# Batch 0's image rows made first from a copy of their own, and the patches of the other rows spread in parts among the first text chunks

## What is computed

```python
h = patches_of(x and four shifted copies) -> [32, 36, 3840]       # layernorm over 3840
h = normed @ W.T + b                                              # 36 image tokens a batch
h = concatenate([h, txt], axis=1)                                 # 164 tokens
# attention on layernorm(h):  k0, v0, g0 are those of batch 0 alone
retrieved = einsum('bhk,hkv->bhv', q_t, fw)
fw = 0.95 * fw + (0.1 * g0_t) * (k0_t outer v0_t)                 # one state for all batches
h = h + layernorm(h) + retrieved @ w_out.T
# experts on layernorm(h): rms norm, router, top 2 of 8
y = sum over the two experts of  down_e(silu(gate_e x) * up_e x) * weight
h = h + layernorm(h) + y
```

## Time and profile before

| | us |
|---|---|
| runs of the kernel: 613.36, 619.07, 621.52; median | 619.07 |
| the profiled execution's own time | 614.67 |
| its span in the trace | 612.9 |
| PE busy in the span | 501.1 (82%) |
| DVE busy | 363.5 (59%) |
| ACT busy | 296.8 (48%) |
| POOL busy | 186.7 (30%) |

### The profile page before, as it was taken

One profiled execution on the slowest core, in us unless ns is written; L12 is line 12 of the kernel. 1 busy time (PEld: TensorE's weight loads), 2 busy tenths in 40 slices (PEclk: granted clock), 3 DMA queues, 4 the chain that ended last, 5 costly groups with the idle time before them and its releaser, 6 DMA issues. The chain is left out here.

```text
span 612.9 us, 12751 instructions
## 1 busy us (share of the span) xinstructions
PE 501.1 (82%) x3132; PEld 469.3 (77%) x3133; DVE 363.5 (59%) x1235; ACT 296.8 (48%) x744; POOL 186.7 (30%) x270
## 2 busy tenths in 40 slices
PE   5999999997887868500999999999999999999300
PEld 2799998876775756400999999999999999999300
DVE  2658855365777655573466565655566665655286
ACT  0268864336567544451344444444444444444262
POOL 0000000005556655552133333333333333333300
PEclk9999999697889786755899999999999999999755
DMA  8992205511223322222222222222222222222299
GB/s 355 435 373 103 104 1 169 194 38 54 78 79 92 95 82 67 84 67 88 51 75 75 75 74 72 67 75 74 75 75 75 75 75 73 65 75 66 94 422 305
DMA packets 52028, 71.62 MB, mean 117 GB/s; under 512 B 18994, under 2 KB 45427, under 8 KB 50467
## 3 DMA queue, kind: packets, MB, share of 16 engines
q1 hardware_dynamic: 39632, 47.93, 24.6%
q0 software_dynamic: 8208, 16.95, 7.7%
q10 hardware_dynamic: 4162, 6.45, 2.8%
HBM read 49.43 MB, written 21.86 MB: 116 GB/s over the span
## 5 line engine op out<-in xcount | busy, mean ns | idle before, releaser
L688 POOL DMA_INDIRECT disp<-xf,posu x82 | 81.7, 997 | 196.5 <-ACT xf L579 164.1
L700 POOL DMA_INDIRECT ydram<-ysb,dnow x89 | 87.3, 981 | 69.4 <-POOL dnow L697 66.4
L1361 DVE TENSOR_TENSOR hh<-sg,bank 128x384 f32<-128x384 f32 x89 | 49.3, 554 | 94.2 <-ACT sg L641 94.2
L641 ACT ACTIVATE sg<-bank 128x384 f32<-128x384 f32 x89 | 43.7, 491 | 114.7 <-PE bank L966 114.7
L962 PE MATMUL bank<-wa,xh 128*128 x178 | 67.7, 380 | 0.0
L966 PE MATMUL bank<-wa,xl 128*128 x178 | 60.5, 340 | 0.0
L964 PE MATMUL bank<-wa,xl 128*128 x178 | 60.4, 339 | 0.0
L963 PE MATMUL bank<-wa,xh 128*128 x178 | 60.2, 338 | 0.0
L965 PE MATMUL bank<-wa,xh 128*128 x178 | 60.0, 337 | 0.0
L697 POOL COPY dnow<-dest 128x1 uint32 (+1 forms) x89 | 16.4, 184 | 123.5 <-DVE ysb L1371 123.5
L868 PE MATMUL pair<-nst,xT 96*128 96x208 f32 x164 | 45.3, 408 | 8.1 <-DVE posu L1264 8.0
(11 more groups left out here) (234 smaller groups left out, 1174.2 us busy)
## 6 DMA issues: line engine op xcount, KB each, us to landing
xs<-disp SPq DMA_DIRECT2D x89, 96.0 KB, 2.0
imgT<-in_pixels SPq DMA_DIRECT2D x4, 1536.0 KB, 17.8
band<-in_bands SPq DMA_DIRECT2D x4, 1536.0 KB, 12.8
yall<-ydram ACTq DMA_DIRECT2D x5, 768.0 KB, 13.2
hres<-in_text SPq DMA_DIRECT2D x1, 3072.0 KB, 34.1
wa<-in_gate_up_w SPq DMA_DIRECT2D x8, 384.0 KB, 8.5
ring<-in_gate_up_w SPq DMA_DIRECT2D x32, 96.0 KB
yall<-ydram SPq DMA_DIRECT2D x4, 768.0 KB, 13.3
```

The costliest lines, as they stand in the source:

```text
L688: pool.indirect_dma_start(disp, bass.IndirectOffsetOnAxis(ap=posu[c % XBUF][:, 2 * j + k:2 * j + k + 1], axis=0), xfd[c % XBUF][:, j, :], None
L700: pool.indirect_dma_start(ydram, bass.IndirectOffsetOnAxis(ap=dnow[b][:], axis=0), ysb[b][:], None).then_inc(s_ys[b], 16)
L1361: v.tensor_tensor(hh[o][:], sg[o][:], bank[2 * o + 1][:, 0:DE], ALU.mult).then_inc(s_hh, 1)
```

## The change

- The host hands over two more inputs: `pixels0`, the pixels of batch 0's 36 image tokens as matmul columns, and `features0`, the same tokens' 3840 features as 36 rows. PE makes the 36 tokens in one group of 24 matmuls with 36 stationary columns; ACT takes their squares in two instructions, and DVE norms them (`t0`, `h0`, `h0n`). With the text rows they give a whole `x0T`, so one projection, one gate and one set of products cover all of batch 0's 164 tokens. `pick`, `head_bank` and the products of the head are gone.
- Before that PE runs three quarters of patch 0, then five parts of 6 matmuls among the first `rows`, and then 7 parts in each of the first four chunks, 3 after the first two `present`, 4 after the last two. The patches go through two PSUM banks in turn, not four.
- The chunks run in the order 3 to 9, 2, 0, 1, 10. The states and rows of chunks 1, 2 (`nsti`) and 0 to 2 (`crowi`) are kept for later.
- The squares, the reading and the norming of patches, the statistics and the norming of tiles move into `turn(t)` of ACT and DVE, t = 0 to 21 by half-chunk. The units run at the turns of `UNIT_TURN`, six of the 28 before turn 9, the other 22 from turn 9 on. SP's loads are reordered around that.
- Some constants are set by POOL rather than DVE, and buffers are laid elsewhere (`wcT`, `aw`, `xs`, `x0`).

The core of the diff:

```diff
-EARLY = (0, 1, 2, 5, 6)
-LATE = (3, 4, 7, 8)
-PATCH_BANK = (0, 1, 5, 6)
-PROJ_BANK = (4, 7, 2, 3)
+PATCH_BANK = (2, 3)
+PROJ_BANK = (4, 6, 5, 7)
+ORDER = (3, 4, 5, 6, 7, 8, 9, 2, 0, 1, 10)
+LN_GROUPS = (range(12, 20), range(20, 28), range(28, 36), range(36, 41), range(8, 12), range(0, 8))
+STATS_TURN = (None, 0, 3, 7, 9, 10)
+PART = 6
+READ_TURN = (None, 0, 2, 3, 4, 5, 6, 7, 8)
+UNIT_TURN = (4, 4, 5, 6, 6, 7, 9, 9, 9, 10, 10, 11, 11, 12, 12, 13, 13, 14, 14, 15, 15, 16, 16, 17, 17, 18, 19, 21)
...
 @block.sync
+            sp.dma_start(img0[:], pixels0).then_inc(s_img0, 16)
+            sp.dma_start(feat0[:], features0).then_inc(s_feat0, 16)
...
+            sp.wait_ge(s_sq, 12)
+            sp.dma_start(band[0][:], bands[:, 2]).then_inc(s_band[2], 16)
+            sp.wait_ge(s_pat, 3)
+            main_in(EXPERTS[0])
...
 @block.scalar
+            def turn(t):
+                if t:
+                    add_norm(turn_norms(t))
+                if t + 1 < PTILES:
+                    squares(t + 1)
+                if t < PTILES:
+                    std_patch(t)
+                if t in STATS_TURN:
+                    std_text(STATS_TURN.index(t))
+                for n in turn_units(t):
+                    high(n)
...
+            for i in range(CHUNKS):
+                c = ORDER[i]
+                if i + 1 < CHUNKS:
+                    xT_out(i + 1, 0)
+                turn(2 * i)
+                if i + 1 < CHUNKS and nt(i + 1) > 2:
+                    xT_out(i + 1, 1)
+                if i > 1:
+                    norm2(i - 1)
+                if IMAGES <= c < CHUNKS - 1:
+                    state_out(c + 1)
+                turn(2 * i + 1)
...
+                if i:
+                    add_norm2(i - 1)
+                std2(i)
...
 @block.tensor
+            def patches(n):
+                for _ in range(n):
+                    p, part = divmod(next(part_n), PARTS_OF_PATCH)
+                    i, j = p // 3, p % 3
+                    if part == 0:
+                        pe.wait_ge(s_img[min(j, 1) if i == 0 else i + 1], 16)
+                        if p >= 2:
+                            pe.wait_ge(s_patout, p - 1)
...
+            for k in range(24):
+                ins = pe.matmul(bank[0][0:NPATCH, 0:193], img0[:, k, :], wcT[:, k, :], start=(k == 0), stop=(k == 23))
...
+            patches(3)
+            pe.wait_ge(s_x0n, 2)
...
+            patches(1)
+            pe.wait_ge(s_kvout, NH)
+            pe.wait_ge(s_vvout, NH)
+            rows(0)
...
                 last.then_inc(s_o, 1)
+                if i < 4:
+                    patches(3)
...
+                if i < 4:
+                    patches(4)
...
 @block.vector
+            def turn(t):
+                if 0 < t <= PTILES:
+                    patch_norm(t - 1)
+                if t in READ_TURN:
+                    patch_read(READ_TURN.index(t))
+                if t < PTILES:
+                    patch_var(t)
+                if t in STATS_TURN:
+                    stats1(STATS_TURN.index(t))
+                if t - 1 in STATS_TURN:
+                    scale1(STATS_TURN.index(t - 1))
...
+            for i in range(CHUNKS):
+                turn(2 * i)
+                for n in turn_units(2 * i):
                     low(n)
+                residual(i)
+                sums(i)
+                picks(i)
+                stats_2(i)
+                turn(2 * i + 1)
+                if i + 1 < CHUNKS:
+                    mask(i + 1)
+                places(i)
+                for n in turn_units(2 * i + 1):
                     low(n)
+                scale2(i)
```

More of the change, by code:

```diff
@@ L105, in link, with build @@
         self.wait()
-def build(nc, pixels, bands, text, W, bias, attn_w, par, norm_w, router_w, gu_w, down_w, consts, out):
+def build(nc, pixels, bands, pixels0, features0, text, W, bias, attn_w, par, norm_w, router_w, gu_w, down_w, consts, out):
     with ExitStack() as ctx:
@@ L530, in _ @@
+            act.wait_ge(s_vh0, 1)
+            nc.scalar.activation(p0[:, 10:11], p0[:, 9:10], ACT.Sqrt, bias=cst[0:NPATCH, C_EPS:C_EPS + 1]).then_inc(s_sdh0, 1)
+            for n in range(2):
+                key_projection(n)
+            nc.scalar.preload_act_table_set("sigmoid_and_others")
+            for h in range(4):
+                keys(h)
             act.wait_ge(s_gs, 1)
             nc.scalar.activation(kgate[:], gsum[:], ACT.Sigmoid).then_inc(s_g8out, 1)
+            for h in range(4, NH):
+                keys(h)
@@ L777, in turn @@
-            def turn(c, half):
-                tiles = range(4 * c + 2 * half, 4 * c + min(nt(c), 2 * half + 2))
+            pe.wait_ge(s_wqc, 1)
+            for hp in range(4):
+                for which in range(2):
+                    kv(which, hp)
+            def turn(i, half):
+                tiles = [tile(i, j) for j in range(2 * half, min(nt(i), 2 * half + 2))]
                 pe.wait_ge(s_h1, 1 + max(NORMED.index(t) for t in tiles))
-                if c or half:
-                    pe.wait_ge(s_xT, 2 * c + half)
+                if i or half:
+                    pe.wait_ge(s_xT, 2 * i + half)
@@ L833, in _ @@
-            text_kv(1, 1)
-            for m in range(2):
-                ins = pe.matmul(bank[3][:, 0:SPAD], wgR[:, m, :], x0T[:, m, :], start=(m == 0), stop=(m == 1))
-            ins.then_inc(s_g8, 1)
-            turn(0, 0)
-            text_kv(1, 2)
-            text_kv(1, 3)
-            for which in range(2):
-                pe.wait_ge((s_k0head, s_v0head)[which], 1)
-                pe.wait_ge(s_vvout, 6 + 2 * which)
-                for hp in range(4):
-                    head_kv(which, hp)
@@ L887, in _ @@
+            rows(0)
+            pe.wait_ge(s_st0, 1)
+            turn(0, 0)
+            patches(1)
+            rows(1)
+            state(0)
             turn(0, 1)
-            pe.wait_ge(s_kvout, NH + 2)
-            pe.wait_ge(s_vvout, NH + 2)
-            rows(0)
+            patches(1)
+            rows(2)
+            state(1)
             scores(0)
-            rows(1)
-            pe.wait_ge(s_st0, 1)
-            for c in range(CHUNKS):
-                if c + 1 < CHUNKS:
-                    turn(c + 1, 0)
+            patches(1)
@@ L897, in _ @@
+            rows(3)
+            state(2)
+            patches(1)
+            rows(4)
+            for i in range(CHUNKS):
+                c = ORDER[i]
+                if i + 1 < CHUNKS:
+                    turn(i + 1, 0)
                 pe.wait_ge(s_ns, c + 1)
                 pe.wait_ge(s_rows, 2 * c + 2)
[L899 to L905 removed]
@@ L922, in _ @@
+                if i + 1 < CHUNKS and nt(i + 1) > 2:
+                    turn(i + 1, 1)
+                if nt(i) > 2:
+                    if i:
+                        pe.wait_ge(s_pos, i)
+                    past(i, 2)
+                    present(i, 2)
+                    past(i, 3)
+                    present(i, 3).then_inc(s_o, 1)
+                if i < 4:
+                    patches(4)
+                if IMAGES <= c < CHUNKS - 1:
                     state(c)
-                if c + 2 < CHUNKS:
+                if IMAGES <= c < CHUNKS - 2:
@@ L1046, in _ @@
             v.tensor_copy(rwsc[:], router).then_inc(s_ns, 1)
-            st.link(v.tensor_copy(zrow[:, D + 1:DROW], cst[:, C_PAD:C_PAD + 2]))
-            mean, var, q = (sd2[:, 25 + k:26 + k] for k in range(3))
-            def patch_out(p):
+            st.wait()
+            st.mark(v.scalar_tensor_tensor(out=t0[:], in0=scb[0:NPATCH, 0, :], scalar=p0[:, 3:4], in1=bank[0][0:NPATCH, 0:D],
+                                           op0=ALU.mult, op1=ALU.add))
+            v.wait_ge(s_psd0, 1)
```

793 lines of the change are left out of this document (367 added, 426 removed).

## The result

The changed kernel took 634.75 us in the median of four runs (628.41 to 637.81), the kernel before 618.51 beside it (613.36 to 621.52): a ratio of 1.026, 95% interval 1.015 to 1.037. The profiled execution took 633.23 us, its span 631.4, against 614.67 and 612.9. So it is slower; whether by 2% isn't settled by these runs. Beside 585.7 the changed kernel took 613.5, a ratio of 1.050 (1.045 to 1.055).

A forecast was written before the change was run, and what follows sets the result against it. No engine is full in the chunks; PE, fullest up to the fifth router sums, was followed with waits for others. Last router sums at 274.9 instead of 266.8, 8.1 us later, on 614.67 give 622.8 us; range 600 to 636.

The forecast's parts named there:

- the case of no change or a little slower: Whole kernel: last chunk's router sums 8.1 us later, 622.8 us; the forecast itself, chance 0.50.
- z0 to z4: From the first chunk's router sums, at 88.0 us, to the fifth's, at 189.9: four periods with patch parts.
- Up to z0: Head until the first chunk's router sums: batch 0's patch 8.0 us, projection from 38.0, first router sums at 88.0.
- Waits for banks: Chunks 1 to 3 of the loop: PE waits for DVE to read patches from two banks, 11.4 us, between 0 and 18.
- Third period: Third to fourth router sums: patches 5 and 6 wait 3.8 and 2.1 us for banks, period 28.4 us.
- The fourth period: Fourth to fifth router sums: ACT's roots 17.6 us after `present`, then DVE's work, 23.0 us in all.
- z4 and z5: Fifth and sixth router sums at 189.9 and 208.4 us; the period between is DVE's, 18.5 us.
- Last chunks: Chunks without patches after the sixth router sums: 13.8 us each, tenth router sums at 263.4, last at 274.9.
- Rival of the filled holes: Chunks: ACT and DVE are as early as PE needs, so bank waits go: 601.1 us; chance 0.22.
- Rival of the longer scatter round: Late chunks: moved units lengthen the scatter's round to 15.9 us, four times 2.1 us more: 631.3 us; chance 0.20.
- Rival of the clock: Patch parts in the loop: bank waits bring PE's clock to 0.83, 18 us longer: 641 us; chance 0.08.

The follow-up runs named there:

- the early reading: Changed kernel with DVE reading every patch from 2 on out of its bank as soon as it is there: 601.19 us, ratio 1.029.
- second profile: Changed kernel run again unchanged in a later group, beside a kernel before at the 585 level: 613.50 us, ratio 1.050.
- ACT's list put in order: Changed kernel with banks read early, tiles normed before the state, second-layer roots earlier, text roots last in their turn, residual update later: 596.61 us, ratio 1.021.
- the experiment without parts: Changed kernel with the remaining 28 patch parts all run ahead of the first chunk, with DVE's and ACT's share: 638.05 us, ratio 1.089.
- the version with earlier patches: Changed kernel, ACT's list reordered, patches two turns further ahead, 12 parts instead of 5 before the loop: 620.30 us without interval; 617.6 us, ratio 1.005.

## Why the prediction was right, and where its steps were off

The time, 622.8 forecast, was 633.2 in the profiled execution, inside the range of 600 to 636 and near its upper end; the case of no change or a little slower was right in sign and 10 us short. The difference to the kernel before is a harder test: forecast 8.1 us, measured 16 in the medians of the first group and 28 at 585, where 13.8 us a chunk, the base of the sum, isn't the kernel's own pace. That the time fell into the range is in part luck of the level at which it was first taken.

By the marks, forecast and measured: z0 to z4 101.9 and 107.9 us, in periods 26.3, 28.4, 24.2 and 23.0 against 26.2, 29.4, 26.5 and 25.8.

- **Up to z0**: 88.0 forecast, 90.2 measured. Batch 0's patch took 9.5 us on PE at a clock of 0.84 and 8.06 at 1.00 (8.0 taken, 7 to 10 given), so the size was right and the clock was left out. z0 is 90.2 in both profiles, though the projection begins at 39.4 in one and at 37.8 in the other, for 38.0 forecast: in the second all of the 2.2 lies in the keys and rows behind it. That narrow stationary columns would not shorten the patch was right: its 48 matmuls took 327 ns in the median, the wide ones 326. The rule on weight loads by their columns, in the Trainium skill's "TensorE: Matmul & The Clock Gate", section LDWEIGHTS, shows in the load in part: 113 ns for 36 columns instead of 189 for 128, shorter, but not in proportion. The load didn't set the pace, so nothing of it reached the time. The experiment that leaves out 18 matmuls shows that the patch is on the path.
- **Waits for banks**: 3.8, 3.8, 2.1 and 1.7 us forecast, 11.4 in all; measured 3.0, 4.5, 1.3 and 1.85, 10.7 in all, and the early reading took 12.3 us off. (The terms that I listed for ACT in the second period add up to 15.7, not 16.3; the copy of the state itself, 0.5, isn't among them.) Mechanism and size were right: the step in which the read stands behind `scale2` and the norming. What a wait does to the clock was not in the sum: 1.75 us in the second period, which came out 1.0 longer than forecast.
- **Third period**: PE went from one last `present` to the next in 24.3 us, as forecast; DVE's router sums came 2.3 us later behind it, after two low units of which the first had waited 1.6 us for ACT.
- **The fourth period** is the step that failed. I let z4 follow ACT's roots by way of DVE, and had no wait of PE for normed tiles. Without holds (second profile) it took 20.6 us, less than forecast: PE waits 4.0 for tiles that ACT norms behind the residual's update and the roots, and z4 comes 0.7 us behind PE's last `present`. In the first profile a hold of 5.2 us on ACT's copy of the state came on top. ACT's list put in order, with the tiles ahead, took the period to 18.1.
- **z4 and z5**: the fifth period took 20.8 us, 18.5 forecast. DVE is busy 17.4 us of it, by the pieces I listed; moving some of its units moved the time into the period before.
- **Last chunks**: 56.5 us for four, 55.0 forecast; the last 9.1 instead of 11.5. This agreement is luck: the 13.8 a chunk was 9.8 of the kernel's own and 4 of holds. At 585 the changed kernel takes 45.5 us for the four and the kernel before 39.3. The sum of the terms: 2.2 + 6.0 + 2.3 + 1.5 - 2.4 = 9.6 us, which is 284.5 - 274.9.
- **Rival of the filled holes**: it needed a kernel before with holes of its own. The waits of ACT and DVE in its 13.8 us a chunk, which I read as room for patches, aren't there at 585 us: 9.8 a chunk, with 1.3 of PE free. Even with the bank waits gone the changed kernel stayed 2.9% slower.
- **Rival of the longer scatter round**: no. POOL's gaps from one chunk's last issue to the next one's first were 5.3, 3.6, 2.0 and 0.3 us between z5 and z10, not over 5.5 throughout.
- **Rival of the clock**: not at its size, 0.94 from z0 to z4. It fell to 0.76 behind z4, and to 0.73 over the first five periods of the experiment without parts. By the section "HAM oscillation" of the same page of the Trainium skill a loop that waits between its bursts pays in each round; the trace agrees for the chunks without parts. Of the first three periods with parts it bears it out in one (0.94, the others 1.00).

Why no gain at all, at 585 us, where both kernels are free of holds: z0 moves up by 42.9 us (133.1 - 90.2), for 50 us of patch parts taken out of the head; the 7 that are missing are about what batch 0's own patch costs. The parts then cost 50 us between z0 and z4, and 6 more come of waits and the clock (101.0 - 45.0 = 56.0). The fifth period adds 10.5, z5 to z9 6.3, the last gives back 0.4: -42.9 + 56.0 + 10.5 + 6.3 - 0.4 = 29.5, and z10 moved by 29.4, from 234.75 to 264.13. Work was moved from a stage in which PE was full into one in which PE had 1.3 us in 9.8 to give; what came with it (batch 0 twice, statistics and units that can't start before the last patch has freed its memory) was extra. With banks and ACT in order 12.4 us are left at z10 (247.2 against 234.75): z4 then comes 4.9 us earlier than in the kernel before (173.2 against 178.1), and what follows takes 17.3 longer.

What stays open: where the holds come from and what divides the two levels; whether the version with earlier patches is level at 585 us too; what the later turns of the units cost by themselves; how much of the late periods is units and how much statistics. No version beat the kernel before.

## What to carry to other kernels

Before work is moved to start a later stage sooner, add up what the fullest engine has to do in both stages together: here PE was busy 190.8 of the 213 us from 21.4 to z10 at 585, so some 22 were free, and no order of the same work could bring more than that, and 7 of them went to a second patch. An engine's waits in a profile are room only if they recur in another run of the same kernel; a wait whose releaser is not an engine of the kernel is the first to be doubted. When two engines' work is woven into a third one's holes, put what the third waits for (bank reads, normed tiles, roots) ahead of everything that nobody waits for: that was worth 17 of the 28 us lost at 585.

## What the runs showed of the hardware

Where holds show, ACT and DVE mostly go on 1.0 to 1.9 us behind the last scatter of a row of eight (the earlier trace rows has 217.65 to 219.32), although PE had long delivered: 13 of the 17 rows with a remote releaser in the chunks of the two first profiles lie so, one comes 0.04 us behind it, three within the row. In the changed kernel PE's state matmuls are over at 177.9 and its scores near 180.4; the last scatter is issued by 181.5:

```profile
177.04 0.84 PE L922 MATMUL bank<-crow,arow 128*96 128x200 f32 x4
...
178.44 1.96 PE L899 MATMUL bank<-xT,keysT 96*128 96x512 f32 x4
...
180.55 0.96 POOL L763 DMA_INDIRECT disp<-xf,posu  x1 [0.31 <-issue]
...
183.08 0.49 ACT L602 COPY nst<-bank 96x400 f32<-96x400 f32 x1 [10.85 <-remote]
183.23 0.69 DVE L1230 TENSOR_TENSOR sm<-bank,cst 128x512 f32<-128x512 f32 x1 [1.76 <-remote]
183.47 0.98 ACT L544 ACTIVATE hres<-hres,lt 128x192 f32<-128x192 f32 x2
...
184.51 0.67 PE L879 MATMUL bank<-ident,hres 128*96 128x128 f32 x4 [4.10 <-ACT hres L544]
```

ACT's copy of the state starts 5.2 us after PE's matmul. DVE's own work, which waits for no other engine, runs on through the scatters. The kernel before shows 41.2 us of such waits, ACT's and DVE's together, in one profile and none in another whose span is 30 us shorter. In both, a scatter takes 0.96 us in the median with 0.30 behind it, so the scatters themselves are no slower where holds show. What holds the engines is open. I had read the waits as part of the kernel.
